# A post-norm attention block with a routed low-rank FFN on one core: group loop written out, last stage as one pipeline

## The chip, the cores and the metric

One core of one Trainium2 chip runs the whole program in one launch. The metric is the device time in microseconds (us). The kernel before takes 2026.87 us, the median of three runs (2025.49 to 2027.67). The execution that the profiler recorded took 2023.68 us; from its first instruction to its last are 2021.7 us (the span), and 2.0 us lie around that.

## What is computed

The reference, cut to what matters (one sequence of 1024 rows, width 512, 32 query heads of 128, 8 key/value heads):

```python
q, k, v = x @ w_q, x @ w_k, x @ w_v            # 32, 8 and 8 heads of 128
lk, lv = (x @ w_lq) @ w_lk, x @ w_lv           # 32 latent heads
q, k, lk = rope(q), rope(k), rope(lk)
attn = causal_softmax(q k^T * SCALE) v         # k, v shared by 4 heads
lat  = causal_softmax(q lk^T * SCALE) lv
x = layernorm(x + attn @ w_o + lat @ w_lo)
logits = x @ route_w.T                         # 8 experts
route_weight = one_hot(argmax(logits)) * max(logits)
h  = x @ A                                     # 8 experts x rank 16 = 128 columns
x = layernorm(x + (route_weight * h) @ Bw)
```

## The kernel before

The work before the last stage goes over 8 groups (one key/value head each, `GROUPS`) and in each over 2 pairs of query heads (`PAIRS`). Products are made in three matmuls of high and low parts (helper `three`, lines 349 to 351). For each pair the kernel projects and rotates queries and latent keys, and then goes over 32 score tiles of 128 rows: TensorE makes scores and transposes probabilities (line 435), VectorE takes row maxima (line 782) and low parts (line 724), ScalarE exponentials and high parts (line 551), GpSimd normalises probabilities (line 712) and makes low parts of weights (line 688). At a pair's end `outputs` multiplies the heads' results by `w_o` and `w_lo` for 8 row tiles of 128 rows (12 matmuls each); VectorE adds each to `acc`, which holds the residual, from PSUM (line 831).

The loop over the groups is a loop of the hardware on each engine (`sp.Fori`, `pe.Fori` and so on, line 486 for TensorE): the body stands in the program once, at its end is a compare and a branch, and the counts to wait for are worked out by register instructions from the group's number. Each engine runs its own list of instructions in the order in which the code writes them; semaphores join the lists. Nothing else orders the work.

What stands behind the loop, the last stage, runs in sections. VectorE waits until all 8 row tiles have been added, takes mean and variance of rows (`bn_stats`, line 845, `bn_aggr`, line 844), and makes 1/sqrt(variance + eps) from ScalarE's square root (line 643) by a reciprocal and one Newton step, four small instructions (lines 858 to 862), in two halves of 4 row tiles. It normalises the row tiles itself (line 870). TensorE transposes them (line 521), ScalarE copies that to SBUF (line 650), and TensorE makes logits and `h` together, 136 columns a row (line 529). When all 8 are there, VectorE makes the routing weights for the 8 row tiles in seven small instructions (lines 893 to 899) and weighs `h` (line 901). TensorE transposes the weighed rows (line 539), ScalarE copies (line 657), TensorE multiplies by `Bw` (line 544), VectorE adds (line 908), and the second norm goes as the first, again in two halves. SyncE stores each row tile when it is finished (line 340).

## Time and profile before

| | |
|---|---|
| median of the runs | 2026.87 us |
| the profiled execution | 2023.68 us |
| its span | 2021.7 us |
| TensorE busy with matmuls | 1979.0 us (98%), 12640 matmuls |
| VectorE busy | 1356.1 us (67%) |
| GpSimd busy | 1129.1 us (56%) |
| ScalarE busy | 1054.6 us (52%) |
| mean granted TensorE clock | 0.994 |
| chain that ended last | TensorE 97%, VectorE 1%, issue 1% |

Busy time counts instructions at work on data. Matmuls overlap, so the start of one to the start of the next says more than a duration: a matmul of 512 columns has a duration of 0.39 us, and the next starts 0.23 us after it. The last of the loop's matmuls starts at 1971.70 us, and the last stage fills the rest of the span.

### The profile page before, as it was taken

The numbers are of one execution on the slowest core, as the hardware profiler recorded it, in microseconds if no ns is written. First come the engines' busy times: TensorE is split into PE (matmuls) and PEld (weight loads), VectorE is DVE, ScalarE is ACT, GpSimd is POOL, SyncE is SP. The second block draws the span as 40 slices with busy tenths as digits, with TensorE's granted clock in tenths as the row PEclk, the third lists the DMA queues.
The fourth block names the chain that finished last, engine by engine and source line by source line (L and its number), as shares of the span: only waits on it lengthen the run. The fifth ranks groups of instructions, "written<-read, shape, count | busy, mean of one in ns | idle before, by whom it ended". The sixth has DMA issues, their size and how long they took to land.

```text
span 2021.7 us, 39463 instructions
## 1 busy us (share of the span) xinstructions
PE 1979.0 (98%) x12640; PEld 1806.8 (89%) x12640; DVE 1356.1 (67%) x3356; ACT 1054.6 (52%) x2445; POOL 1129.1 (56%) x905
## 2 busy tenths in 40 slices
PE   7999999999999999999999999999999999999994
PEld 6989989899898989989899898999989899898993
DVE  6758667585775747758476675757757586675756
ACT  3746627375372745728356372654727366272641
POOL 6637476374664647556465664646566374763730
PEclk9999999999999999999999999999999999999997
DMA  5010010101000010000100001010010100100001
GB/s 177 12 35 1 23 36 12 35 1 43 15 22 24 2 57 1 22 24 3 55 1 22 24 22 36 1 45 1 23 36 12 35 1 23 36 13 21 2 12 42
DMA packets 19366, 50.85 MB, mean 25 GB/s; under 512 B 5824, under 2 KB 7872, under 8 KB 19008
## 3 DMA queue, kind: packets, MB, share of 16 engines
q1 hardware_dynamic: 18992, 45.90, 6.8%
q8 instruction: 119, 1.95, 0.4%
q10 hardware_dynamic: 144, 2.10, 0.2%
q14 instruction: 111, 0.91, 0.2%
HBM read 45.89 MB, written 2.10 MB: 24 GB/s over the span
## 4 chain that ended last, share of the span: by engine, by line
PE 97%; DVE 1%; issue 1%; POOL 0%; DVEq 0%; POOLq 0%; ACT 0%; ACTq 0%
PE ps L349 28%; PE ps L350 28%; PE ps L351 28%; PE ps L435 13%; DVE stats L845 0%; PE ps L529 0%; PE ps L544 0%; PE ps L521 0%; DVE acc L870 0%; POOL pt_lo L688 0%; DVE acc L908 0%; DVE stats L844 0%; POOL mask L678 0%; DVE neg_max L782 0%; DVE acc L831 0%
## 5 line engine op out<-in xcount | busy, mean ns | idle before, releaser
L712 POOL TENSOR_TENSOR probs<-probs,inv_sum 128x640 f32<-128x640 f32 (+7 forms) x512 | 582.9, 1150 | 343.9 <-DVE inv_sum L789 342.9
L782 DVE CUSTOM_DVE_ANT_0 probs<-ps,mask 128x640 f32<-128x640 f32 (+7 forms) x512 | 384.3, 753 | 167.2 <-PE ps L351 121.1
L724 DVE TENSOR_TENSOR pt_lo<-ps,pt_hi 128x512 fp32r<-128x512 f32 (+3 forms) x768 | 399.0, 547 | 75.1 <-ACT pt_hi L551 73.2
L551 ACT ACTIVATE pt_hi<-ps 128x512 fp32r<-128x512 f32 (+3 forms) x768 | 347.0, 487 | 164.0 <-PE ps L435 160.8
L580 ACT ACTIVATE probs<-probs,neg_max 128x640 f32<-128x640 f32 (+7 forms) x512 | 397.0, 776 | 60.5 <-DVE neg_max L782 49.3
L349 PE MATMUL ps<-pt_hi,val_hi 128*128 128x256 f32 x1216 | 353.8, 291 | 0.0
L350 PE MATMUL ps<-pt_lo,val_hi 128*128 128x256 f32 x1216 | 342.7, 282 | 0.0
L351 PE MATMUL ps<-pt_hi,val_lo 128*128 128x256 f32 x1216 | 342.5, 282 | 0.0
L435 PE MATMUL ps<-ident,probs 128*128 128x128 f32 x2304 | 334.4, 273 | 0.0
L703 POOL TENSOR_TENSOR probs<-probs 128x512 f32<-128x512 f32 x144 | 186.7, 1296 | 198.9 <-DVE probs L758 198.9
L435 PEld LDWEIGHTS ps<-ident,probs 128*128 128x128 f32 x2304 | 271.9, 140 | 23.6
L551 ACT ACTIVATE ql_hi<-probs 128x512 fp32r<-128x512 f32 x128 | 80.9, 632 | 403.5 <-POOL probs L703 403.5
L350 PEld LDWEIGHTS ps<-pt_lo,val_hi 128*128 128x128 f32 x1216 | 232.2, 191 | 0.6
L349 PEld LDWEIGHTS ps<-pt_hi,val_hi 128*128 128x128 f32 x1216 | 231.9, 191 | 0.6
L351 PEld LDWEIGHTS ps<-pt_hi,val_lo 128*128 128x128 f32 x1216 | 231.6, 190 | 0.0
L688 POOL TENSOR_TENSOR pt_lo<-raw,pt_hi 128x1024 fp32r<-128x1024 f32 (+1 forms) x48 | 96.8, 2030 | 241.2 <-ACT pt_hi L551 241.2
L349 PE MATMUL ps<-val_hi,ql_hi 128*128 128x512 f32 x512 | 202.7, 396 | 0.0
L351 PE MATMUL ps<-val_hi,ql_lo 128*128 128x512 f32 x512 | 199.7, 390 | 0.0
L350 PE MATMUL ps<-val_lo,ql_hi 128*128 128x512 f32 x512 | 199.6, 390 | 0.0
L831 DVE TENSOR_TENSOR acc<-ps,acc 128x512 f32<-128x512 f32 x128 | 85.3, 688 | 153.4 <-PE ps L351 153.4
L724 DVE TENSOR_TENSOR ql_lo<-ps,ql_hi 128x256 fp32r<-128x256 f32 x256 | 105.0, 414 | 106.7 <-ACT ql_hi L551 103.3
L707 POOL TENSOR_TENSOR ql_lo<-probs,ql_hi 128x512 fp32r<-128x512 f32 x128 | 166.5, 1300 | 7.8 <-ACT ql_hi L551 7.8
(100 smaller groups left out, 4025.6 us busy)
## 6 DMA issues: line engine op xcount, KB each, us to landing
raw<-wo SPq DMA_DIRECT2D x32, 512.0 KB, 3.4
raw<-wq SPq DMA_DIRECT2D x16, 512.0 KB, 3.8
raw<-wlv SPq DMA_DIRECT2D x16, 512.0 KB, 3.6
raw<-wkv SPq DMA_DIRECT2D x8, 512.0 KB, 3.6
acc<-xT SPq DMA_DIRECT2D x4, 512.0 KB, 6.2
wlk_raw<-wlk SPq DMA_DIRECT2D x16, 128.0 KB, 3.0
acc<-x ACTq DMA_DIRECT2D x1, 2048.0 KB, 8.8
out<-acc SPq DMA_DIRECT2D x8, 256.0 KB, 2.4
```

Of the source, the lines that this page charges most:

```text
L349: pe.matmul(dst, ah, bh, start=first, stop=False, skip_group_check=True)
L350: pe.matmul(dst, ah, bl, start=False, stop=False, skip_group_check=True)
L351: return pe.matmul(dst, al, bh, start=False, stop=last, skip_group_check=True)
L435: mm = pe.transpose(ps[:, T_BANKS[u % len(T_BANKS)], P * (b - b0):P * (b - b0) + P], probs_of(n)[:, P * b:P * b + P], ident[:])
L551: return nc.scalar.activation(dst, src, ACT.Copy)
L580: nc.scalar.activation(dst, dst, ACT.Exp, bias=neg_max[:, n % 8:n % 8 + 1], scale=-1.0, accum_out=row_sum[:, n % 8:n % 8 + 1]).then_inc(q[ ...
L688: nc.gpsimd.tensor_tensor(l, raw_part(name), h, ALU.subtract).then_inc(q["w_lo_pool"], 1)
L703: nc.gpsimd.tensor_tensor(b[:, 0:512], b[:, 0:512], b[:, 512:1024], ALU.add).then_inc(q["rope_add"], 1)
L707: nc.gpsimd.tensor_tensor(l, probs[:, slot_of_rope(pair, r - 1), 0:512], h, ALU.subtract).then_inc(q["rope_lo"], 1)
L712: nc.gpsimd.tensor_tensor(b, b, inv_sum[:, k % 8:k % 8 + 1].to_broadcast([P, b.shape[-1]]), ALU.mult).then_inc(q["normed"], 1)
L724: return nc.vector.tensor_tensor(dst, src, h, ALU.subtract)
L782: nc.vector.tensor_tensor_reduce(out=probs_of(n).rearrange("p (b n) -> p b n", b=b), in0=scores_of(n), in1=mask[:, S - w:S].rearrange("p ( ...
```

## The change

Four things change:

- `Fori` becomes a Python `for`: the 8 groups stand in the program one after the other on all five engines. There is no branch, and each wait has a constant, so the register instructions are gone.
- The rows are taken in the order in which their outputs come (`OUT_ORDER`, `row(y)`), in three batches (`BATCHES`): y = 0 to 3, 4 and 5, 6 and 7. Norm, logits, routing and FFN of a batch start when that batch is there. The last two outputs (y = 6, 7) of the last pair are taken out of the loop and stand in pieces between the steps of the first batch.
- Rows are normalised by ScalarE (`normalize`: activation Identity with a bias and a scale for each partition), in place of VectorE's instruction of line 870. VectorE makes the bias, -mean/std, in one more small instruction for each batch (`scale6`).
- Buffers in PSUM: x and weighed rows are transposed into banks 4 and 5; logits and `h` go to banks 6, 7, 2, 3; FFN products to 0, 1, 6, 7. The copy of the logits to SBUF (line 893) is dropped; the routing reads PSUM.

The diff, cut:

```diff
-LN_TILES = ST // 2
+BATCHES = ((0, 1, 2, 3), (4, 5), (6, 7))
...
-            with pe.Fori(0, GROUPS) as g:
+            for g in range(GROUPS):
...
+                        if (g, pair) == (GROUPS - 1, PAIRS - 1) and y == 6:
+                            break
...
+            turn_x1(0, "pt_lo_made", GROUPS * PAIRS * T_UNITS)
+            turn_x1(1, "pt_lo_made", GROUPS * PAIRS * T_UNITS)
+            outputs(*last, 6, 0, 1)
+            mix(0)
+            turn_x1(2, "x1T_made", 1)
+            mix(1)
+            turn_x1(3, "x1T_made", 2)
+            outputs(*last, 6, 1, 2)
+            mix(2)
+            mix(3)
+            outputs(*last, 6, 2, 4)
+            outputs(*last, 7, 0, 2)
+            turn_wh(0, "x1T_made", 3)
+            turn_wh(1, "x1T_made", 4)
+            turn_x1(4, "whT_made", 1)
+            turn_x1(5, "whT_made", 2)
+            outputs(*last, 7, 2, 4)
+            ffn(0)
+            ffn(1)
+            turn_wh(2, "x1T_made", 5)
+            turn_wh(3, "x1T_made", 6)
+            mix(4)
+            mix(5)
+            ffn(2)
+            ffn(3)
+            turn_wh(4, "whT_made", 3)
+            turn_wh(5, "whT_made", 4)
+            turn_x1(6, "whT_made", 5)
+            turn_x1(7, "whT_made", 6)
+            ffn(4)
+            mix(6)
+            mix(7)
+            ffn(5)
+            turn_wh(6, "x1T_made", 7)
+            turn_wh(7, "x1T_made", 8)
+            ffn(6)
+            ffn(7)
...
+            def normalize(norm, y):
+                act.wait_ge(q[f"chain{norm}"], 6 * (batch_of(y) + 1))
+                nc.scalar.activation(row(y), row(y), ACT.Identity, bias=shift[:, y:y + 1], scale=rstd[:, y:y + 1]
+                                     ).then_inc(q["x1_made" if norm == 1 else "finished"], 1)
```

Of the helpers, `turn_x1(y)` is 4 transposes, `mix(y)` the 4 matmuls for logits and `h`, `turn_wh(y)` one transpose, `ffn(y)` the product with `Bw`; on VectorE `add_last(y)` and `add_ffn(y)` are the adds into `acc`, `spread` is `bn_stats`, `moments` the `bn_aggr` of a batch with the eps added, `scale1` to `scale6` and `route1` to `route6` are single small instructions, and `weigh(y)` is the product with the routing weights.

On TensorE the loop's end before: the last matmuls of the body, the branch, and then the last stage, all transposes and `mix`.

```order
L349 MATMUL ps<-val_hi,ql_hi 128x512
L350 MATMUL ps<-val_lo,ql_hi 128x512
L351 MATMUL ps<-val_hi,ql_lo 128x512
L486 REGISTER_ALU
L486 COMPARE_AND_BRANCH
L521 MATMUL ps<-ident,acc 128x128 [waits x1_made]
L521 MATMUL ps<-ident,acc 128x128 x3
L521 MATMUL ps<-ident,acc 128x128 [waits x1_made]
L521 MATMUL ps<-ident,acc 128x128 x3
L521 MATMUL ps<-ident,acc 128x128 [waits x1T_made,x1_made]
L521 MATMUL ps<-ident,acc 128x128 x3
L529 MATMUL ps<-raw,probs 128x136 [waits x1T_made,out_added,ffn_in]
```

In the changed program the first group's last matmuls are followed at once by the second group's first (`x_hi` with the query weights):

```order
L385 MATMUL ps<-val_hi,ql_hi 128x512
L386 MATMUL ps<-val_lo,ql_hi 128x512
L387 MATMUL ps<-val_hi,ql_lo 128x512
L385 MATMUL ps<-x_hi,pt_hi 128x512 [waits w_lo_pool]
L386 MATMUL ps<-x_lo,pt_hi 128x512
L387 MATMUL ps<-x_hi,pt_lo 128x512
L385 MATMUL ps<-x_hi,pt_hi 128x512
```

The branch is gone. Further on, behind the outputs of y = 5 of the last pair, TensorE has the first transposes of normalised rows, with the three matmuls of one step of y = 6 in between:

```order
L385 MATMUL ps<-val_hi,ql_hi 128x512
L386 MATMUL ps<-val_lo,ql_hi 128x512
L387 MATMUL ps<-val_hi,ql_lo 128x512
L557 MATMUL ps<-ident,acc 128x128 [waits pt_lo_made,x1_made]
L557 MATMUL ps<-ident,acc 128x128 x3
L557 MATMUL ps<-ident,acc 128x128 [waits pt_lo_made,x1_made]
L557 MATMUL ps<-ident,acc 128x128 x3
L385 MATMUL ps<-val_hi,ql_hi 128x512 [waits out_added]
L386 MATMUL ps<-val_lo,ql_hi 128x512
L387 MATMUL ps<-val_hi,ql_lo 128x512
L568 MATMUL ps<-raw,probs 128x136 [waits x1T_made,o_lo_made,ffn_in]
L568 MATMUL ps<-raw,probs 128x136 x3
```

All 24 matmuls of the outputs of y = 6 and 7 now stand behind the first transposes of normalised rows.

On VectorE before, behind the 8 adds of the last pair, stand the statistics of a half:

```order
L798 REGISTER_ALU
L798 COMPARE_AND_BRANCH
L845 BN_STATS stats<-acc 128x6 [waits out_added]
L845 BN_STATS stats<-acc 128x6 x3
L844 BN_AGGR stats<-stats 128x2 [waits ln_chain]
L844 BN_AGGR stats<-stats 128x2 x3
L852 TENSOR_SCALAR ve<-stats 128x4 [waits ln_chain]
L845 BN_STATS stats<-acc 128x6 x4
L844 BN_AGGR stats<-stats 128x2 [waits ln_chain]
L844 BN_AGGR stats<-stats 128x2 x3
L852 TENSOR_SCALAR ve<-stats 128x4 [waits ln_chain]
L858 RECIPROCAL rstd<-root 128x4 [waits root_made]
```

In the changed program the same engine, at the place where the second batch's routing begins (y = 7's add `L914`, FFN adds `L956`, statistics `L961`):

```order
L914 TENSOR_TENSOR acc<-ps,acc 128x512 [waits out_mm]
L961 BN_STATS stats<-acc 128x6 [waits out_added]
L956 TENSOR_TENSOR acc<-ps,acc 128x512 [waits y_mm] x2
L961 BN_STATS stats<-acc 128x6 [waits y_added] x2
L914 TENSOR_TENSOR acc<-ps,acc 128x512 [waits out_mm]
L961 BN_STATS stats<-acc 128x6 [waits out_added]
L1015 TENSOR_REDUCE top<-ps 128x2 [waits route,logits_mm]
L968 BN_AGGR stats<-stats 128x2 [waits stats1]
L968 BN_AGGR stats<-stats 128x2
L970 TENSOR_SCALAR ve<-stats 128x2 [waits moments1]
L1020 TENSOR_TENSOR cos_t<-ps,top 128x16 [waits route]
L984 RECIPROCAL rstd<-root 128x2 [waits chain1,root1]
```

The add of y = 7 and its statistics now stand behind the first two FFN adds and their statistics, and the second batch's routing (`L1015`, `L1020`) and the third batch's norm (`L968`, `L970`, `L984`) are laced together.

On ScalarE before, the last stage: a table load, two roots, copies, two roots.

```order
L643 ACT_TABLE_LOAD
L643 ACTIVATE root<-ve 128x4 [waits ve_made] x2
L650 ACTIVATE probs<-ps 128x512 [waits x1_turned] x6
L650 ACTIVATE probs<-ps 128x512 [waits logits_mm,x1_turned] x2
L657 ACTIVATE probs<-ps 128x128 [waits wh_turned,logits_mm]
L657 ACTIVATE probs<-ps 128x128 [waits wh_turned]
L657 ACTIVATE probs<-ps 128x128 [waits y_mm,wh_turned] x6
L643 ACTIVATE root<-ve 128x4 [waits ve2_made] x2
```

In the changed program, the part from the third batch's first root to the second norm's second root (`L721` is `normalize`, `L728` and `L734` are the copies):

```order
L734 ACTIVATE probs<-ps 128x128 [waits wh_turned] x2
L728 ACTIVATE probs<-ps 128x512 [waits x1_turned] x2
L717 ACTIVATE root<-ve 128x2 [waits ve1]
L734 ACTIVATE probs<-ps 128x128 [waits wh_turned]
L734 ACTIVATE probs<-ps 128x128 [waits y_mm,wh_turned] x3
L721 ACTIVATE acc<-acc,shift,rstd 128x512 [waits chain1] x2
L728 ACTIVATE probs<-ps 128x512 [waits logits_mm,x1_turned] x2
L717 ACTIVATE root<-ve 128x4 [waits ve2]
L734 ACTIVATE probs<-ps 128x128 [waits y_mm,wh_turned] x2
L717 ACTIVATE root<-ve 128x2 [waits ve2]
L721 ACTIVATE acc<-acc,shift,rstd 128x512 [waits chain2] x4
```

Roots, copies and normalised rows are laced on one engine. The root that waits for `ve1` now stands ahead of the copies that TensorE's FFN products wait for.

## Rows read from the trace of the kernel before

**Rows 1.** Busy time by stretches of the end; columns: stretch, length, engines, clock, DMA.
```profile
1972.10:1980.40 8.30, 0.00 (x0) 0.00 (x0) 7.93 (x26) 0.41 (x2) 0.00 (x0) 0.65 0.00 0
...
2009.00:2018.60 9.60, 0.05 (x1) 0.00 (x0) 9.03 (x28) 0.20 (x1) 0.00 (x0) 0.67 0.35 130
```
**Rows 2.** What TensorE waited for: total us, times, longest us.
```profile
PE ps L521 <- DVE acc L870: 8.4, 1, 8.4
...
PE ps L349 <- issue: 3.5, 7, 0.9
PE ps L349 <- POOL pt_lo L688: 2.6, 1, 2.6
```
**Rows 3.** TensorE in order of time, one branch: start, duration, instruction, idle before.
```profile
751.71 0.39 PE L350 MATMUL ps<-val_lo,ql_hi 128*128 128x512 f32 x1
751.94 0.39 PE L351 MATMUL ps<-val_hi,ql_lo 128*128 128x512 f32 x1
752.60 0.49 PE L349 MATMUL ps<-x_hi,pt_hi 128*128 128x512 f32 x1 [0.27 <-issue]
752.93 0.39 PE L350 MATMUL ps<-x_lo,pt_hi 128*128 128x512 f32 x1
```
**Rows 4.** Busy time by stretches: one without a branch; TensorE is first.
```profile
510.00:750.00 240.00, 239.70 (x1547) 220.14 (x1546) 163.25 (x405) 129.75 (x302) 140.91 (x112) 1.00 0.06 20
```
**Rows 5.** TensorE in order of time, the last stage.
```profile
1966.48 0.39 PE L349 MATMUL ps<-val_hi,ql_hi 128*128 128x512 f32 x1
...
1986.33 0.60 PE L521 MATMUL ps<-ident,acc 128*128 128x128 f32 x4
1986.77 1.09 PE L529 MATMUL ps<-raw,probs 128*128 128x136 f32 x8
...
1997.83 1.02 PE L544 MATMUL ps<-raw,probs 128*128 128x512 f32 x2
1998.69 0.27 PE L539 MATMUL ps<-ident,raw 128*128 128x128 f32 x1
```
**Rows 6.** VectorE in order of time, the last stage.
```profile
1957.89 1.88 DVE L831 TENSOR_TENSOR acc<-ps,acc 128x512 f32<-128x512 f32 x3
...
1972.85 2.47 DVE L845 BATCH_NORM_STATS2 stats<-acc 128x6 f32<-128x512 f32 x4
...
1979.04 0.16 DVE L859 TENSOR_TENSOR newton<-rstd 128x4 f32<-128x4 f32 x1
1979.24 0.16 DVE L860 TENSOR_TENSOR newton<-newton,ve 128x4 f32<-128x4 f32 x1
...
1994.11 0.22 DVE L894 TENSOR_REDUCE top<-cos_t 128x8 f32<-128x64 f32 x1
...
1995.65 1.67 DVE L901 TENSOR_TENSOR raw<-ps,cos_t 128x128 f32<-128x128 f32 x8
...
2016.65 1.91 DVE L870 TENSOR_SCALAR acc<-acc,stats,rstd 128x512 f32<-128x512 f32 x4
```
**Rows 7.** ScalarE's groups by shape: busy us, mean ns of one, idle before.
```profile
L551 ACT ACTIVATE ql_hi<-probs 128x512 fp32r<-128x512 f32 x128 | 80.9, 632 | 403.5 <-POOL probs L703 403.5
...
L580 ACT ACTIVATE probs<-probs,neg_max 128x512 f32<-128x512 f32 x64 | 46.1, 720 | 17.1 <-DVE neg_max L782 17.1
...
L650 ACT ACTIVATE probs<-ps 128x512 f32<-128x512 f32 x8 | 4.8, 598 | 7.7 <-PE ps L521 7.7
L657 ACT ACTIVATE probs<-ps 128x128 f32<-128x128 f32 x8 | 2.1, 277 | 9.4 <-PE ps L539 9.4
...
L643 ACT ACTIVATE root<-ve 128x4 f32<-128x4 f32 x4 | 0.8, 205 | 29.4 <-DVE ve L852 29.4
```
**Rows 8.** Busy time by stretches around the second norm; the clock is the number behind POOL's.
```profile
2002.90:2005.40 2.50, 0.01 (x1) 0.01 (x1) 2.43 (x9) 0.48 (x2) 0.00 (x0) 1.00 0.01 3
2005.40:2008.80 3.40, 3.38 (x4) 1.17 (x4) 1.16 (x2) 0.00 (x0) 0.00 (x0) 0.50 0.00 0
```
**Rows 9.** The page's DMA queues: packets, MB, share of 16 engines.
```profile
q8 instruction: 119, 1.95, 0.4%
```

More of the change, by code:

```diff
@@ L485, in _ @@
             pe.wait_ge(q["lq_lo_made"], 2)
[L486 removed]
+            for g in range(GROUPS):
                 for pair in range(PAIRS):
@@ new lines, in mix @@
+            def mix(y):
+                if y == 0:
+                    pe.wait_ge(q["ffn_in"], 32)
+                    pe.wait_ge(q["o_lo_made"], GROUPS * PAIRS * CHUNKS)
+                if y in (4, 6):
+                    pe.wait_ge(q["out_added"], SEED + GROUPS * PAIRS * ST - ST + (7 if y == 4 else 8))
+                pe.wait_ge(q["x1T_made"], y + 1)
+                for c in range(CT):
+                    mm = pe.matmul(mix_of(y), turned_x1(y)[:, P * c:P * c + P], ra[:, c, :], start=c == 0 and y % 2 == 0,
+                                   stop=c == CT - 1 and y % 2 == 1, skip_group_check=True)
+                mm.then_inc(q["logits_mm"], 1)
@@ new lines, in turn_wh, with ffn @@
+            def turn_wh(y, free, count):
+                pe.wait_ge(q["wh_made"], y + 1)
+                pe.wait_ge(q[free], count)
+                pe.transpose(ps[:, 4 + y % 2, 0:P], raw[:, 2, P * y:P * y + P], ident[:]).then_inc(q["wh_turned"], 1)
+            def ffn(y):
+                if y < 2:
+                    pe.wait_ge(q["out_added"], SEED + GROUPS * PAIRS * ST - ST + 5 + y)
+                elif y >= 4:
+                    pe.wait_ge(q["y_added"], y - 3)
+                pe.wait_ge(q["whT_made"], y + 1)
+                pe.matmul(y_of(y), turned_wh(y), raw[:, 1, 0:D], start=True, stop=True).then_inc(q["y_mm"], 1)
@@ L603, in _ @@
             nc.scalar.dma_start(acc[:], x).then_inc(q["res_in"], 16)
-            with act.Fori(0, GROUPS) as g:
+            for g in range(GROUPS):
                 for pair in range(PAIRS):
@@ L796, in output_lo, with add_output @@
                 lo(l, product_of(n), h).then_inc(q["o_lo_made"], 1)
-            with dve.Fori(0, GROUPS) as g:
+            def add_output(g, pair, y):
+                dve.wait_ge(q["out_mm"], SEED + per_pair(g, pair, ST, y + 1))
+                nc.vector.tensor_tensor(row(y), ps[:, y % 4, :], row(y), ALU.add).then_inc(q["out_added"], 1)
+            for g in range(GROUPS):
                 for pair in range(PAIRS):
@@ L889, in _ @@
-            chain = [0]
-            dve.wait_ge(q["logits_mm"], ST)
-            mix = ps[:, 4:8, :].rearrange("p b (y n) -> p (b y) n", y=2)
-            logits, equal, ranked, first, weight = (route[:, i] for i in range(5))
-            step(nc.vector.tensor_copy(logits, mix[:, :, 0:E]))
-            step(nc.vector.tensor_reduce(top[:], logits, AX.X, ALU.max))
-            step(nc.vector.tensor_tensor(equal, logits, top[:, :, None].to_broadcast([P, ST, E]), ALU.is_equal))
-            step(nc.vector.tensor_tensor(ranked, equal, order[:, None, :].to_broadcast([P, ST, E]), ALU.mult))
@@ L915, in _, with add_last, add_ffn @@
-            finish(ln2, 1)
+                    if (g, pair) != (GROUPS - 1, PAIRS - 1):
+                        for y in range(ST):
+                            if g == 0 and pair == 0 and y == 0:
+                                dve.wait_ge(q["res_in"], 16)
+                            add_output(g, pair, y)
+            def add_last(y):
+                add_output(GROUPS - 1, PAIRS - 1, y)
+            def add_ffn(y):
+                dve.wait_ge(q["y_mm"], y + 1)
+                nc.vector.tensor_tensor(row(y), y_of(y), row(y), ALU.add).then_inc(q["y_added"], 1)
@@ new lines, in spread, with moments @@
+            def spread(norm, y):
+                dve.wait_ge(q["out_added" if norm == 1 else "y_added"], (SEED + GROUPS * PAIRS * ST - ST if norm == 1 else 0) + y + 1)
+                nc.vector.bn_stats(stats[:, y, 0:6], row(y)).then_inc(q[f"stats{norm}"], 1)
+            def moments(norm, b):
+                ys = in_batch(b)
+                dve.wait_ge(q[f"stats{norm}"], ys.stop)
+                for y in BATCHES[b]:
+                    nc.vector.bn_aggr(stats[:, y, 6:8], stats[:, y, 0:6]).then_inc(q[f"moments{norm}"], 1)
+                dve.wait_ge(q[f"moments{norm}"], ys.stop)
+                nc.vector.tensor_scalar(ve[:, ys], stats[:, ys, 7], EPS, None, ALU.add).then_inc(q[f"ve{norm}"], 1)
@@ new lines, in _ @@
+            spread(2, 1)
+            add_last(7)
+            spread(1, 7)
+            route1(1)
+            moments(1, 2)
+            route2(1)
+            scale1(1, 2)
+            route3(1)
+            scale2(1, 2)
+            route4(1)
+            scale3(1, 2)
+            route5(1)
+            scale4(1, 2)
+            route6(1)
+            scale5(1, 2)
+            weigh(4)
+            scale6(1, 2)
+            weigh(5)
+            add_ffn(2)
+            add_ffn(3)
+            spread(2, 2)
```

356 lines of the change are left out of this document (230 added, 126 removed).

## The prediction

> **What bounds the kernel now.** I read the page's busy shares first: TensorE is busy 98% of the span, and the chain that ended last is 97% TensorE. So up to the last matmul of the loop only two things can move the time: TensorE's work, which the change leaves as it is, and holes in it. Next the waits of TensorE [rows 2] and the busy time by stretches. Over 240 us without a branch TensorE lacks 0.30 us [rows 4]; there is nothing to win there. Seven times, once for each jump back to the loop's head, it stops with the releaser "issue", 3.5 us in all [rows 2]. Then the end: from 1972.1 to 1980.4 TensorE does nothing while VectorE makes the first norm [rows 1], which is the wait of 8.4 us on the normalised rows [rows 2]; from 2009.0 to 2018.6 only VectorE works [rows 1]. The last normalised row is written at 1.91 + 2016.65 = 2018.56 [rows 6], and stores fill the 3.1 us to 2021.7. So the last stage is bound by a chain that goes to and fro between the engines, and the loop by TensorE.
>
> **The change, part by part.**
>
> The branch. The last matmul of a group starts at 751.94 and the next at 752.60 [rows 3]: 0.66 where matmuls of this size follow each other by 0.23 (751.71 to 751.94), so 0.43 lost; the one behind it comes after 0.33, another 0.10. The profile's "idle" of 0.27 there is this 0.43 less the modelled end of a matmul, 0.39 - 0.23 = 0.16. Over seven jumps that makes 3.5 [rows 2] + 7 x (0.16 + 0.10) = 5.3 us. It all stands on the path, since TensorE has its operands. With the code written out there is no jump: -5.3. Bounds: -3.5 (the idle alone) and -5.3 less another 2, if VectorE's, ScalarE's and GpSimd's missing register instructions also shorten the short waits of TensorE inside a group.
>
> The entry. TensorE waits 2.6 us for the first low parts of weights [rows 2]. ScalarE and SyncE set up registers before the instructions that lead there; I take 0.3 off this wait, an estimate between 0 and 0.6. Taken: -0.3.
>
> The end, as a chain in the time of before. Prices, each as the distance from one start to the next when engines are full: add 0.60 (3 in 1.88, the last 0.69 long), `bn_stats` 0.60 (4 in 2.47), small VectorE instructions that follow each other through a semaphore 0.20 (1979.04 to 1979.24), routing instructions 0.22 long, so 0.25, weighing 0.20 (8 in 1.67) [rows 6]. TensorE: 4 transposes 0.44 (1986.33 to 1986.77), `mix` 1.09 long, so 0.93, `ffn` 0.86 (1997.83 to 1998.69) [rows 5], a transpose of a weighed row 0.11, an output's 12 matmuls 12 x 0.23 = 2.72; a result is there some 0.16 after the engine is free. ScalarE: copy of x 0.60, of a weighed row 0.28, root 0.21 [rows 7]; queued ones overlap by about 0.1. From one engine to another 0.04.
>
> The one price that no row shows is ScalarE's normalising instruction, with a pointer for the bias and one for the scale. A copy of 512 columns without pointers takes 0.632, an exponential of 512 with a pointer for its bias 0.720 [rows 7]. One pointer is then 0.088 at most, and a second as much: 0.81, 0.71 when queued. Bounds: 0.54 (VectorE's own in line 870, from 4 in 1.91 [rows 6]) and 0.90. ScalarE's table holds, since the program has no more table loads than before.
>
> The Trainium skill ("ScalarE: Activation LUTs", "What ACT_TABLE_LOAD costs") states 186 ns + 0.833 ns a column, and some 93 ns more for each pointer: 0.80 us here. It speaks against this part of the change, since VectorE does the same in 0.54; the rows agree with its first pointer, and no row of this profile has two. By 0.72, the price of one pointer alone, the end would come 0.9 us earlier than below.
>
> 1. TensorE leaves the outputs of y = 5 at 1966.48 [rows 5]. The outputs of y = 3 left it 2 x 2.72 earlier, at 1961.04, so their add starts at 1961.24; with it, two statistics still due and the moments (0.60 + 1.20 + 0.6) VectorE is at 1963.7, and with the root and six small instructions (0.28 + 6 x 0.20) at 1965.2. ScalarE normalises four rows (4 x 0.71) and copies the first: `mix(0)` starts at 1968.7. TensorE fills all but 0.7 of that with transposes and one step of y = 6.
> 2. From there it is full until `ffn(1)`: 4 mix 3.72, 4 times 4 transposes 1.76, the other 21 output matmuls 4.76, two transposes of weighed rows 0.22, two ffn 1.72, a wait of 0.4 for the copies, 0.2 to the result: 1981.5. The routing of the first batch hides beside the outputs of y = 6 and 7.
> 3. VectorE: adds and statistics of FFN rows 0 and 1 come before the add of y = 7, then its statistics and the third batch's moments: 0.60 + 1.20 + 0.73 + 0.71 + 0.48 = 3.7 (the last is the moments: aggregates and eps, each behind a semaphore), to 1985.2.
> 4. ScalarE's root of the third batch stands ahead of the copies of weighed rows 2 and 3; they and `ffn(2)` wait for it: 0.56, to 1985.8. TensorE is idle for 2.4 us here. This is the wait that the change makes anew.
> 5. `ffn(2)`, `ffn(3)`, two transposes 2.0; two copies and two normalised rows 1.9: 1989.7. Transposes, `ffn(4)`, `mix(6)`, `mix(7)` 3.4: 1993.1. Six routing instructions and one weighing 1.8: 1994.9. Transpose, copy 0.65, `ffn(6)`, `ffn(7)` 1.9: 1997.4.
> 6. Add, two statistics, moments 2.55: 2000.0. ScalarE's root comes behind the normalised rows 0 to 3, then four more, 4 x 0.71: with the root 3.25, to 2003.25.
>
> Against 2018.56: -15.3. The stores stay, 3.1 us behind the last row. Where this gain comes from: the 8.3 and 9.6 us of VectorE alone [rows 1] become about 3 and 6, and in the chain from 1980 to 2009 the batches overlap. Sum: -5.3 - 0.3 - 15.3 = -20.9. The profiled execution's 2023.68 would be 2002.8; the median of the runs stands 3.2 above it, so **2006.0** is predicted.
>
> **Rivals.**
>
> *The clock falls in the new hole.* Before, TensorE stood idle for 2.5 us at a granted clock of 1.00, and the next 3.4 us, though full, were at 0.50 [rows 8], so 1.2 instead of 2.4 GHz. Step 4's hole is 2.4 us. For it: length. Against: the stretch of rows 8 came at the end of a stage in which TensorE had waited for others again and again; here it is full for over 14 us ahead of the hole (steps 1 and 2) and has 2 us of work right behind it. A stretch of 3.4 us at half rate, of which the matmuls on the chain are half, costs 1 to 2 us: about 2007.6.
>
> *More from the loop.* All register instructions on VectorE's and GpSimd's chains go; if TensorE's short waits inside the groups shrink with them, up to 2 us more: 2004.2. Against: rows 4 leave 0.30 us idle in 240.
>
> *Slower: straight code pays for fetching.* If each block of instructions fetched cost TensorE's queue what a jump costs, 119 fetches [rows 9] less the 8 at the loop's ends, by 5.3/7 = 0.76 each, would add 84 us: 2006 + 84 = 2090. It turns the result from 20.9/111 = 0.19 us a fetch. Against: a turn of the loop has 12640/8 = 1580 matmuls with as many weight loads, these packets are fetched in each turn of the loop already, and rows 4 have a full TensorE over them.
>
> *No gain at the end.* If the laced stage ran at half clock throughout, my chain would be 16 us longer, and 5.6 us of the branch and the entry remain less 0.7: 2022. Against: before the stage TensorE is full, and has only short holes in it.
>
> **How the numbers follow.** Forecast 0.62; clock falls once or twice 0.24; more from the loop 0.07; half clock throughout 0.03; fetching 0.02; 0.02 for a wait I have not seen. Runs of this kernel lie within 2.2 us, so 0.2% (4.1 us) is what can be told from no change. Faster: the first three and most of the last, 0.94. Same: half clock and the like, 0.03. Slower: 0.03. The range is the forecast with its bounds (1.9 less or 1.1 more for the normalising instructions, 2 either way for the branch, 2 for the handoffs between engines, of which the chain has some 25 at 0.04, in case one costs twice that and more), widened to the clock's case: 2002.0 to 2010.5.
>
> **What would show it.** Right: no "issue" among TensorE's waits; TensorE idle by less than 1 us between the last `outputs` and `mix`, one hole of 2 to 2.5 us behind `mix(5)` released by ScalarE's copy, and holes of about 1.3 and 1.2 ahead of `turn_x1(6)` and `turn_wh(6)`; Identity of 512 columns at 0.80; ScalarE full in the last 3 us before the last store. Wrong: TensorE losing starts at other places of the straight code; a clock of 0.5 in the stretch of the outputs of y = 6 and 7; a normalising instruction over 0.90; a span over 2006 or under 1997.

## The result and the profile after

The changed kernel takes **2005.88 us**, the median of four runs (2004.14 to 2007.88). The kernel before, run beside it, takes 2026.44 (2025.49 to 2027.67). The ratio is 0.9899 with a 95% interval of 0.9881 to 0.9916, so the change makes the kernel 20.6 us, or 1.0%, faster. The forecast was 2006.0 for the time and 20.9 for the gain. The time is inside the range and "faster" had 0.94.

The profiled executions tell less of a gain: 2023.68 before and 2007.88 after, with spans of 2021.7 and 2005.8. That is 15.9 and not 20.9, and the recorded limit for a wrong prediction, a span over 2006, was all but reached. Most of this text is on those 5 us.

The page after, for the waits and code loads that stood in [rows 2] and [rows 9]. First TensorE's waits (total us, times, longest us):

```profile
PE ps L385 <- DVE x_lo L838: 7.9, 1, 7.9
PE ps L385 <- POOL pt_lo L802: 4.7, 1, 4.7
PE ps L583 <- ACT probs L734: 2.1, 1, 2.1
...
PE ps L557 <- ACT acc L721: 1.1, 1, 1.1
PE ps L575 <- DVE raw L1048: 0.8, 1, 0.8
PE ps L568 <- ACT probs L728: 0.6, 1, 0.6
```

"Issue" is gone, and so is the 8.4 us wait on VectorE's normalised rows. The wait for the first low parts of the weights, 2.6 in [rows 2], is 4.7. The 2.1 us on ScalarE's copy in line 734 is the new hole that step 4 of the prediction named. Code loading, the queue of [rows 9] (packets, MB, share):

```profile
q8 instruction: 102, 1.67, 0.3%
```

102 packets against 119: the written-out program did not load more on this queue. The same 240 us of the middle as in [rows 4] (stretch, length, TensorE's busy time, and the other engines behind it):

```profile
510.00:750.00 240.00, 239.72 (x1547) 220.19 (x1546) 163.56 (x405) 129.57 (x302) 140.82 (x112) 1.00 0.06 21
```

TensorE lacks 0.28 us there and lacked 0.30 before. And a place where one group ends and the next begins, which answers to [rows 3] (start, duration, instruction):

```profile
752.89 0.39 PE L386 MATMUL ps<-val_lo,ql_hi 128*128 128x512 f32 x1
753.11 0.39 PE L387 MATMUL ps<-val_hi,ql_lo 128*128 128x512 f32 x1
753.34 0.39 PE L385 MATMUL ps<-x_hi,pt_hi 128*128 128x512 f32 x1
753.57 0.39 PE L386 MATMUL ps<-x_lo,pt_hi 128*128 128x512 f32 x1
```

The starts are 0.23 apart all the way through. With the jump, the last matmul of the group and the first of the next were 0.66 apart.

The last stage, TensorE in order of time (the number in brackets is idle time and what ended it); it answers to [rows 5]:

```profile
1978.08 1.88 PE L583 MATMUL ps<-raw,probs 128*128 128x512 f32 x4
1979.80 0.38 PE L575 MATMUL ps<-ident,raw 128*128 128x128 f32 x2
1980.02 2.02 PE L568 MATMUL ps<-raw,probs 128*128 128x136 f32 x16
1984.15 3.68 PE L583 MATMUL ps<-raw,probs 128*128 128x512 f32 x4 [2.11 <-ACT probs L734]
...
1989.17 1.36 PE L557 MATMUL ps<-ident,acc 128*128 128x128 f32 x8 [1.12 <-ACT acc L721]
...
1994.87 0.53 PE L575 MATMUL ps<-ident,raw 128*128 128x128 f32 x2 [0.78 <-DVE raw L1048]
```

The same four instructions of line 583, `ffn`, take 1.88 us at 1978.08 and 3.68 behind the hole at 1984.15. The clock tells why (stretch, length, TensorE, its loads, VectorE, ScalarE, GpSimd, then the granted clock):

```profile
1981.95:1984.10 2.15, 0.09 (x1) 0.00 (x0) 1.89 (x9) 0.38 (x3) 0.00 (x0) 1.00 0.00 0
1984.15:1987.60 3.45, 3.45 (x4) 1.35 (x5) 1.95 (x12) 0.11 (x1) 0.00 (x0) 0.51 0.00 0
```

TensorE stood idle at a granted clock of 1.00 and then worked at half of it, 1.2 GHz in place of 2.4. This is the first rival, "the clock falls in the new hole"; it happened in this execution.

ScalarE from there to the end, with line 721 the normalising, 717 the root and 734 the copies of weighed rows:

```profile
1983.72 0.20 ACT L717 ACTIVATE root<-ve 128x2 f32<-128x2 f32 x1 [6.18 <-DVE ve L970]
1983.83 0.42 ACT L734 ACTIVATE probs<-ps 128x128 f32<-128x128 f32 x2
...
1996.97 2.91 ACT L721 ACTIVATE acc<-acc,shift,rstd 128x512 f32<-128x512 f32 x4
2000.20 0.20 ACT L717 ACTIVATE root<-ve 128x2 f32<-128x2 f32 x1 [0.31 <-DVE ve L970]
```

The root that waits for VectorE until 1983.7 stands ahead of two copies whose transposes TensorE had finished by 1980.2 (1979.80 and 0.38 above), 3.5 us sooner. Before, VectorE normalised these rows, and the last stage ended with [rows 6]. Of the instruction that no row had priced, the group by shape (busy us, mean ns | idle before):

```profile
L721 ACT ACTIVATE acc<-acc,shift,rstd 128x512 f32<-128x512 f32 x16 | 11.8, 802 | 1.3 <-DVE shift L1009 1.2
```

0.802 us against 0.81 forecast, and the queued distance is (2.91 - 0.80)/3 = 0.70 against 0.71. The Trainium skill ("ScalarE: Activation LUTs", "What ACT_TABLE_LOAD costs") states 186 ns and 0.833 ns a column, and some 93 ns for each pointer, which makes an estimate of 0.80; this trace agrees.

### The profile page after: what moved, and what is told of

Same layout as the page of the kernel before. It is cut to its first block, busy times and chain, and to the rows that moved or that the text cites. A ratio compares the mean times of both kernels' runs of the same rounds, so it can differ in the third digit from the quotient of the medians.

```text
span 2005.8 us, 33652 instructions
## 1 busy us (share of the span) xinstructions
PE 1977.5 (99%) x12640; PEld 1806.8 (90%) x12640; DVE 1352.0 (67%) x3369; ACT 1064.1 (53%) x2463; POOL 1128.6 (56%) x905
## 4 chain that ended last, share of the span: by engine, by line
PE 88%; POOL 5%; DVE 4%; ACT 2%; issue 1%; SPq 1%; DMA 0%; ACTq 0%; DVEq 0%; POOLq 0%
PE ps L385 25%; PE ps L387 25%; PE ps L386 25%; PE ps L471 13%; POOL probs L817 3%; POOL ql_lo L821 2%; DVE probs L871 1%; DVE probs L870 1%; DVE probs L872 1%; ACT probs L656 1%; PE ps L583 0%; SPq L349 0%; ACT ql_hi L627 0%; DVE probs L896 0%; DVE val_lo L838 0%
## 5 line engine op out<-in xcount | busy, mean ns | idle before, releaser
L914 DVE TENSOR_TENSOR acc<-ps,acc 128x512 f32<-128x512 f32 x128 | 85.4, 687 | 144.2 <-PE ps L387 144.2
```

## Where the two profiled executions differ

Both spans cut at the same four places: the twelfth matmul of the loop over (the thirteenth starts), the start of the last matmul of the outputs of y = 5, the end of the last normalised row, the end. Each is read from the trace's instructions, in us from the start of the span.

| | before | after | difference | forecast |
|---|---|---|---|---|
| entry: to 12 matmuls into the loop | 23.01 | 26.03 | +3.0 | -0.3 |
| loop: from there to y = 5 | 1943.24 | 1938.42 | -4.8 | -5.3 |
| last stage: to the last row | 52.30 | 38.94 | -13.4 | -15.3 |
| stores | 3.1 | 2.4 | -0.7 | 0 |
| span | 2021.7 | 2005.8 | -15.9 | -20.9 |

The mechanism and the order of the sizes are there. Two things were against the changed kernel: an entry that is 3 us later, and 1.7 us lost to the clock behind the hole. Half of the 3 us is the clock too: the first matmul of the loop starts at 21.65 in place of 20.12, and the first twelve take 4.38 in place of 2.89. Theory A says that the late entry is a matter of the single execution, and that the profile of before had fallen on an early one (it lay 2.8 under the median of its runs). Theory B says that straight code makes the entry late, and a third possibility was that the load of x collides with the weights. The first four experiments and the second profile of before are for these.

## Experiments

All numbers are medians with the range of the runs in brackets, the ratio to the kernel before on the same chip with its 95% interval, and parts by the cuts of the table above. The kernel before had a median of 2025.81 beside the first four, of 2023.72 beside the four on the last stage's bound and the entry's loads, and of 2026.33 beside the last two, so medians from different groups are not comparable to better than 2 to 3 us; the parts read from the traces are.

**The changed kernel a second time, its two halves, and one load later.** No edit:

> The changed kernel once more, unaltered. Its profiled execution was 15.9 us shorter in span than the kernel before's, where 20.9 was forecast; 3.2 of the 5.0 us between lie at the entry: the first weights landed 1.4 us later than before, TensorE waited 4.7 us in place of 2.6 and then ran 3.4 us at the granted clock 0.50. Theory A (the entry is chance: which of the loads lands first): in this execution TensorE may wait under 3 us at the entry with the clock at 1.00, and then the span is near 2002; the times spread by 3 to 4 us. Theory B (the straight code makes the entry slower): TensorE waits over 4 us here too, and the span is near 2005.5.

Measured: 2005.66 (2004.12 to 2008.46), ratio 0.9906 [0.9891, 0.9922], span 2002.2. Its entry is over at 23.70, the last stage takes 37.25, and the clock doesn't fall behind the hole. The same code gives a span 3.6 us shorter: 2.3 of it is the entry and 1.7 the clock behind the hole, less 0.4 in the loop. Of theory A's two signs at the entry one came: the wait is 2.96, but the clock fell there too, 1.5 us behind the first matmul. The hole in the last stage is as long as in the first profile, but what follows is at full rate (columns as above):

```profile
1980.00:1982.10 2.10, 0.08 (x1) 0.00 (x0) 1.84 (x9) 0.33 (x3) 0.00 (x0) 1.00 0.00 0
1982.20:1985.60 3.40, 2.27 (x7) 1.03 (x8) 3.25 (x15) 1.39 (x5) 0.00 (x0) 1.00 0.00 0
```

The straight code alone, on the kernel before (the edit is the same on all five engines; besides, VectorE's wait for the load of x stands only in the first pair, as in the changed kernel):

```diff
-            with pe.Fori(0, GROUPS) as g:
+            for g in range(GROUPS):
```

> Only the five group loops are written out, the last stage is the kernel before's. The forecast's term for the seven jumps is 5.3 us, all on TensorE: no wait with the releaser issue is left, and the stretch from the first matmul of the first group to the last matmul of the last group is 5.3 us shorter (1951.58 us before, 1946.3 here), at whatever the entry costs. Theory A: 2021 us when the entry is as before, 2024 when the weights land late, so between 0.9973 and 0.999 of before. Theory B: the entry costs 3 us more each time, 0.999. A third, that straight code also shortens waits inside the groups, would make the stretch under 1945.

Measured: 2021.42 (2016.28 to 2025.14), ratio 0.9977 [0.9967, 0.9988], 4.4 us under the 2025.81 of before. Its loop takes 1938.41, as the changed kernel's, its last stage 52.8; its entry is over at 25.74.

The new end alone, with the loop kept over seven groups and the eighth, the same code, written behind it (on all five engines):

```diff
-            for g in range(GROUPS):
+            def group(g):
...
+            with pe.Fori(0, GROUPS - 1) as g:
+                group(g)
+            group(GROUPS - 1)
```

> The last stage of the change, with a hardware loop over the first seven groups and only the last group written out, so six jumps are left. By the forecast's terms the last stage gives 15.3 us and one jump 0.76, against before -16.1: 2010.4 us, and 4.5 us more than the changed kernel at an equal entry. The waits with the releaser issue are 6, some 3.0 us in all. If the gain were in the straight code, it would be near before. Theory B on the entry: the first wait is about 2.6 us here as in the kernel before, since the loop's code is the same there; theory A: it varies as in the others.

Measured: 2010.09 (2007.76 to 2012.03), ratio 0.9921 [0.9908, 0.9935], 15.7 under before. Its entry is over at 25.38, with a wait of 2.60. Six jumps are left and cost as before (total, times, longest):

```profile
PE ps L390 <- issue: 3.4, 6, 0.8
```

The halves give 4.4 and 15.7, together 20.1, and the whole kernel beside them 20.15. One jump, 0.6 to 0.8, is gone in both, and each interval is 2 to 3 us to either side; within that they add up, and neither hides the other.

The load of x into the accumulators, which starts at 15.3, put behind the weights of the first group:

```diff
-            nc.scalar.dma_start(acc[:], x).then_inc(q["res_in"], 16)
...
                     weights_hi(g, f"lv{pair}")
+                    if g == 0 and pair == 0:
+                        nc.scalar.dma_start(acc[:], x).then_inc(q["res_in"], 16)
```

> The changed kernel with ScalarE's load of the residual x (2 MB) put behind its high parts of the first pair's weights, so it no longer runs beside the first loads of weights. If that load is what makes the first weights land late (the memory queues moved 440 GB/s from 18 to 22 us in the changed kernel), they land by 16 us, TensorE's wait at the entry is under 3 us, the clock stays at 1.00, and the span is 2001 to 2002.5, the times 1 to 3 us under the changed kernel's with less spread. If the queue of loads ahead of them or the straight code is the cause, nothing changes: 2005.

Measured: 2006.37 (2003.95 to 2007.39), ratio 0.9901 [0.9886, 0.9916]; that load now starts at 20.5, the wait for the first low parts is 4.6 all the same, and the entry is over at 25.76. That load isn't what makes the weights late.

**Is the entry the straight code's?** The kernel before once more, with a profile:

> The kernel before, unchanged, profiled a second time. Its first twelve matmuls of the loop were over at 23.0 us of the span in the profile of the prediction, and at 23.7 to 26.2 in all six others with the same loads, one of which keeps the loops. Theory A (the entry is a matter of which transfers land first, the same for both kernels, and the first profile fell on an early one): this one has them over at 24 to 26, waits 3 to 4.7 us for the first low parts, and its time is 1 to 3 us above the 2023.68 of the first profiled execution. Theory B (straight code makes the entry later): again 23 and a wait of 2.6.

Measured: 2025.64 (2023.92 to 2027.19), ratio 1.0004 [0.9994, 1.0014] to itself; the profiled execution took 2026.23. The entry is over at 25.48, 2.5 later than in the profile that the prediction was made from. The first matmul of the loop in the first profile, in this one and in the changed kernel's first, and the stretch that begins there in this one:

```profile
20.12 0.50 PE L349 MATMUL ps<-x_hi,pt_hi 128*128 128x512 f32 x1 [2.65 <-POOL pt_lo L688]
21.08 0.79 PE L349 MATMUL ps<-x_hi,pt_hi 128*128 128x512 f32 x1 [2.60 <-POOL pt_lo L688]
21.65 0.76 PE L385 MATMUL ps<-x_hi,pt_hi 128*128 128x512 f32 x1 [4.67 <-POOL pt_lo L802]
```

```profile
21.00:24.40 3.40, 3.32 (x8) 2.64 (x9) 1.02 (x2) 0.14 (x1) 3.40 (x5) 0.50 0.96 343
24.40:27.00 2.60, 2.60 (x13) 2.12 (x12) 1.30 (x2) 0.00 (x0) 2.15 (x1) 0.99 0.82 298
```

The expectation was half right. The wait is 2.60, as in the first profile and not the 3 to 4.7 expected, but the first matmul comes a microsecond later and at half the clock, where the first profile's was at the full one (its first matmul took 0.50 us, this one 0.79). The length of the wait spoke for theory B: it is 2.60 to 2.65 in the three profiles with loops and 2.5 to 4.7 in the eight without (those with the tables first). But theory B's consequence, a late entry with straight code, falls: the entry of the kernel before is as late as the changed kernel's (23.70, 25.06 and 26.03 in its three profiles), and in the kernel with loops and the new end it was 25.38. The traces also show what the start of the first matmul hangs on. ScalarE makes the high part of the first query weights when these have landed and it is done with the high parts of the latent query, whichever is later; TensorE's first matmul follows 3.55 us later with loops and 3.7 without (us):

| | weights landed | latent query's parts done | ScalarE starts | first matmul | first twelve take |
|---|---|---|---|---|---|
| before, first profile | 16.54 | 16.36 | 16.57 | 20.12 | 2.89 |
| before, second | 16.35 | 17.38 | 17.53 | 21.08 | 4.40 |
| loops with the new end | 16.96 | 17.40 | 17.56 | 21.11 | 4.27 |
| changed, first profile | 17.84 | 15.87 | 17.95 | 21.65 | 4.38 |
| changed, second | 15.90 | 15.65 | 16.01 | 19.72 | 3.98 |
| changed, third | 17.08 | 16.81 | 17.19 | 20.90 | 4.16 |

So the wait is short with loops because the engines reach it later (the latent query's parts are done at 16.4 to 17.4 there, at 15.6 to 16.9 in the eight without), not because the weights land sooner. From this profile of before to the two others of the changed kernel the span falls by 21.9 and 21.0.

**What the last stage is bound by.** The rows normalised by VectorE again, in the new order:

```diff
+            def normalize(norm, b):
+                dve.wait_ge(q[f"chain{norm}"], 6 * (b + 1))
+                for y in BATCHES[b]:
+                    nc.vector.tensor_scalar(row(y), row(y), rstd[:, y:y + 1], shift[:, y:y + 1], ALU.mult, ALU.add
+                                            ).then_inc(q["x1_made" if norm == 1 else "finished"], 1)
```

> The changed kernel with its rows normalised by VectorE (16 TENSOR_SCALAR of 128x512 behind the sixth step of each scale chain, 0.54 us each by [rows of before], 0.48 queued) in place of ScalarE's 16 Identity ACTIVATEs of 0.83. Everything else is the changed kernel's. Theory A (the last stage's gain is the order: a third batch, the last two tiles behind the two short batches, three batches of norm 2): VectorE gets 7.7 us more work in a stage in which it is the engine with the least slack, but each batch saves the hop to ScalarE and 0.35 us a row; worked out through the chain of waits the two cancel, so the time is within 1.5 us of the changed kernel (2004.5 to 2007.5). Theory B (moving the normalising to ScalarE is a large part of the gain): undoing it costs 3 us or more, 2009 or later.

Measured: 2006.96 (2005.54 to 2008.39), ratio 0.9912 [0.9898, 0.9925]. Theory A's range held (its 0.83 for ScalarE's instruction was high, the traces have 0.80). The gain of the end comes from the rest of the new end, its order and batches and buffers; which of the two engines normalises is worth 0.3 to 1.3 us by the medians, which is less than the groups can be compared to. In the trace the last stage takes 40.8, where the first profile's took 38.9; both have the clock down behind the hole of 2.1, and this one a second time, in its last four instructions of `ffn`, which take 3.75 where the first profile's took 1.96, so that most of the 1.9 is the clock's. The price moved to another wait. Four rows of the second norm stand on VectorE ahead of the last weighing, and TensorE waits for that:

```profile
1990.89 1.92 DVE L994 TENSOR_SCALAR acc<-acc,rstd,shift 128x512 f32<-128x512 f32 x4
1992.92 0.49 DVE L1033 TENSOR_TENSOR raw<-ps,cos_t 128x128 f32<-128x128 f32 x2
```

```profile
PE ps L575 <- DVE raw L1033: 2.7, 1, 2.7
```

ScalarE's copies ahead of its root:

```diff
             copy_x1(5)
-            roots(1, 2)
             copy_wh(2)
             copy_wh(3)
+            roots(1, 2)
```

> Only ScalarE's order: the copies of mix tiles 2 and 3 (0.28 us each) ahead of the square root of the third batch, which waits for VectorE until 1983.7. They are ready at 1980.2, so ffn(2) and ffn(3) start without the 2.1 us hole behind mix(5). Theory A (the hole is what the clock falls in, and what stands behind it is bound by VectorE's third batch): the hole goes, with it the 3.4 us at half clock, which cost 1.7; the end moves by 0.6 for the order and up to 1.7 for the clock: 0.6 to 2.3 us earlier than the changed kernel, 2003.5 to 2005.3. Theory B (the end is set by PE's own work behind the hole): all of the 2.1 us and the clock's 1.7 come back, 3.5 us or more, under 2002.5. If the hole is only moved to the next wait (turn_x1(6), for the rows that VectorE's batch gives) the clock can fall there, and the time is the same within 0.6.

Measured: 2005.02 (2004.04 to 2006.54), ratio 0.9907 [0.9892, 0.9922]. By the times that can't be told from no change. By the trace the last stage takes 36.70, against 37.25 in the changed kernel's execution at full clock: 0.55 less, where 0.6 was expected for the order. The hole of 2.11 is gone, and most of it stands again one step on, where TensorE waits for VectorE's weighing:

```profile
1980.45 1.88 PE L583 MATMUL ps<-raw,probs 128*128 128x512 f32 x4
1983.78 0.60 PE L575 MATMUL ps<-ident,raw 128*128 128x128 f32 x2 [1.45 <-DVE raw L1048]
1985.44 1.36 PE L557 MATMUL ps<-ident,acc 128*128 128x128 f32 x8 [1.07 <-ACT acc L721]
```

So the hole showed the wait of the earliest waiter; the bound behind it is VectorE's third batch. This one was attacked next, by moving it ahead of work that isn't due (and, smaller, the routing and statistics around it and ScalarE's rows 6 and 7 ahead of its copies 4 and 5):

```diff
...
             spread(1, 6)
-            add_ffn(0)
-            add_ffn(1)
-            spread(2, 0)
-            spread(2, 1)
             add_last(7)
+            weigh(3)
             spread(1, 7)
-            route1(1)
+            add_ffn(0)
             moments(1, 2)
...
```

> Orders of VectorE and ScalarE alone (TensorE's is the changed kernel's): the last output row 7 is added and its norm and scale chain worked before the first FFN sums, the FFN sums and the statistics of norm 2 fill the waits behind, and ScalarE takes mix copies 2 and 3 ahead of the third square root and the rows 6 and 7 ahead of mix copies 4 and 5. Theory A (the last stage is bound by VectorE's order: row 7's product is ready at 1978.3 and VectorE is idle from 1976.1 to 1979.1, so the third batch's chain can end 2 us sooner, and the holes of 2.1 and 1.1 shrink): the last row ends 3.4 us earlier at full clock, and 1.7 more if the clock no longer falls: 3 to 5 us under the changed kernel, 2001 to 2003. Theory B (TensorE's work is the bound and the holes only move): within 1 us.

Measured: 2002.52 (2000.73 to 2002.89), ratio 0.9889 [0.9874, 0.9904]. The last stage takes 33.7, 3.6 less than the changed kernel's at full clock, against 3.4 expected. The copies' order of the experiment before is in it, 0.55 by itself; the other 3.0 belong to the moves together, which were not tried one by one. TensorE has no hole over 0.8 left in it, and ScalarE's root of the third batch runs at 1980.3 and not at 1983.7:

```profile
1981.38 1.88 PE L583 MATMUL ps<-raw,probs 128*128 128x512 f32 x4
1983.17 0.53 PE L575 MATMUL ps<-ident,raw 128*128 128x128 f32 x2
1984.02 0.63 PE L557 MATMUL ps<-ident,acc 128*128 128x128 f32 x4 [0.32 <-ACT probs L734]
```

```profile
1980.26 0.20 ACT L717 ACTIVATE root<-ve 128x2 f32<-128x2 f32 x1 [0.37 <-DVE ve L970]
```

**The entry.** The weights of the first group stand behind the tables on SyncE's queue. Here the key's and the first query's go ahead, and ScalarE takes the query's high part ahead of those of the latent query:

```diff
-            for slot, table in ((1, cos), (2, sin)):
...
                         sp.dma_start(raw_of(name), src).then_inc(raw_in[i % RAW_SLOTS], 16)
+                        if (g, pair, name) == (0, 0, "q0"):
+                            for slot, table in ((1, cos), (2, sin)):
...
+            weights_hi(0, "q0")
             for n in range(2):
                 act.wait_ge(q["lq_mm"], n + 1)
```

> The changed kernel with the loads of the first key and query weights issued ahead of the four loads of the cos and sin tables (1 MB in 4096 packets of 256 B), and ScalarE's high part of the first query weights ahead of the two of the latent query. Theory A (the entry waits for the first weights because they stand behind the tables on SP's queue): the weights land at about 9 instead of 17.9, the first matmul of the loop is then released by the latent query's low parts at 16.6 or by the tables, 17 to 18 instead of 19.7 to 21.7, and TensorE's idle time of 3.0 to 4.7 shrinks to under 1.5, so that the clock stays up over the first twelve matmuls, which gives another 1.1: 3 to 5 us under the changed kernel, 2001 to 2003. Theory B (the transfers share one rate: what goes ahead pushes the tables back by as much, and the tables' own transposes then wait): 0 to 1.5 us.

Measured: 2001.58 (2000.61 to 2003.03), ratio 0.989 [0.9874, 0.9905]. The median is 4.3 us under the changed kernel's first one, but the kernel before was at 2023.72 on this chip, so the ratios show 2 to 3 us; the last experiment below compares on one chip. The twelfth matmul is over at 20.65, 3 to 5.4 earlier than in the changed kernel's profiles. SyncE's issues in the changed kernel and in this one (start, duration, instruction):

```profile
3.08 3.34 SPq L349 DMA_DIRECT2D probs<-cos  x2
6.46 4.97 SPq L349 DMA_DIRECT2D probs<-sin  x2
11.48 1.20 SPq L353 DMA_DIRECT2D wlk_raw<-wlk  x1
12.72 0.43 SPq L369 DMA_DIRECT2D raw<-wq  x1
```

```profile
3.71 0.64 SPq L365 DMA_DIRECT2D raw<-wq  x1
4.40 1.41 SPq L370 DMA_DIRECT2D probs<-cos  x2
5.85 6.58 SPq L370 DMA_DIRECT2D probs<-sin  x2
```

The weights' load is issued 9 us earlier and lands at 11.6 (expected at about 9), in place of 17.8. What is left is a wait for the tables, the rival's part, of one microsecond (TensorE, in brackets), and the clock stays up behind it:

```profile
16.12 1.94 PE L408 MATMUL ps<-ident,probs 128*128 128x128 f32 x16 [0.97 <-DMA probs<-sin]
```

```profile
21.00:24.40 3.40, 3.40 (x18) 2.85 (x17) 2.84 (x5) 0.00 (x0) 3.40 (x3) 1.00 0.98 410
```

Matmuls of 512 columns start every 0.23 us in it, and every 0.43 at a clock of 0.50 in the second profile of before.

**All of it together**, and the changed kernel beside it. The edits of the last two, and the last row normalised by VectorE in place of ScalarE:

```diff
-            normalize(2, 7)
...
+            nc.vector.tensor_scalar(row(7), row(7), rstd[:, 7:8], shift[:, 7:8], ALU.mult, ALU.add).then_inc(q["finished7"], 1)
```

> The orders of e5_short_batch_first and the loads of e7_weights_first together, and the last row 7 normalised by VectorE (one TENSOR_SCALAR of 0.54) beside ScalarE's row 6. Theory A (the entry and the last stage are apart and add up): e7's 4.3 us and e5's 3.4 us under the changed kernel's median, and 0.7 of the last row by VectorE, 8.4 together: 1997.5 if all of it comes, and span 1994 to 1995. Theory B (the two medians were drawn from one spread of entries, since e5 and e7 were compared with one set of runs of before that was itself lower): the two share 2 us, 1999.5 or later, and the changed kernel run beside it falls under 2004.

Measured: **1997.94** (1997.81 to 2003.21; three of the four runs within 0.3), ratio 0.9869 [0.9853, 0.9886]. Theory A had 1997.5.

> The changed kernel once more, on the chip of the best one. Theory A: 2004 to 2007 as in its first two runs, with an entry that waits 3.0 to 4.7 us for the first weights. Theory B: under 2004. For the clock: of five executions with the 2.1 us hole behind the sixth mix, three fell to half the clock behind it and two did not; this one adds a sixth.

Measured: 2006.71 (2005.15 to 2010.65), ratio 0.9911 [0.9894, 0.9927]; entry over at 25.06, last stage 37.3, no fall of the clock behind the hole. The combination is 8.8 us under the changed kernel on the same chip: by the traces the entry is over 4.1 earlier (20.94) and the last stage is 4.3 shorter (33.0). Theory A holds. With the row on VectorE the last row ends 0.7 sooner than in the experiment with VectorE's new order, and the span gains nothing, for the stores then take 3.14 instead of 2.45.

## Why the prediction was right

*The jumps*, -5.3 forecast. The stretch between entry and last stage is 1943.24 and 1943.82 in the two profiles of before, 1942.98 with six jumps, and 1938.3 to 1938.8 in every kernel without any. That is 4.8 in the profiled pair and 4.4 to 5.5 over all, 0.64 to 0.79 a jump on average against 0.76. Single jumps differ more: counted by starts, as the prediction did for one, the seven of the first profile lose 0.55 to 1.17 each. The working by starts and not by the "idle" column was needed: the idle alone would have given 3.5. Of the 2 us more that the other engines' register instructions might have given nothing came; the rival "more from the loop" is refuted by the lack of 0.28 in 240 us, unchanged.

*The entry*, -0.3 forecast. No run shows a gain from register instructions that is clear of the spread: the latent query's parts are done somewhat earlier without loops, but from ScalarE's first high part to the first matmul it is 3.55 with loops and 3.7 without. What the term missed is the spread. The first profile of before was an early one, with its weights landed at 16.54 and, alone among the eleven profiles in which TensorE waits 2.5 us or more for them, with the clock up over the first twelve matmuls; in the other ten these take 3.98 to 5.26. The prediction had looked for a fall of the clock only in the new hole. Over the others there is no difference between the kernels that the spread of 2 to 3 us would show. The forecast's offset of 3.2 from the profiled execution to the median held this, as the second profile of before suggests (2.5 us later at the entry, 2026.23 in all), so the median came out right although the profiled pair is 5 us off. The term should have been given bounds from below zero to +3.

*The last stage*, -15.3 forecast: from the table's cut the forecast chain takes 37.0 (1966.26 to 2003.25), and measured are 37.2 to 37.3 at full clock and 38.9 with the clock's fall. The holes are at the places named: 0.55 ahead of the first `mix` (0.7 forecast), 2.11 behind `mix(5)` (2.4), 1.12 ahead of `turn_x1(6)` (1.3), 0.78 ahead of `turn_wh(6)` (1.2). The normalising instruction is 0.802 (0.81). Which part of the new end gives how much, the three batches, the outputs of y = 6 and 7 between them or the buffers, was not separated.

*The clock*, a rival with 0.24 and a price of 1 to 2 us. It fell in three of the seven executions profiled with this hole (the first one, with the later load of x, and with VectorE's rows; the expectation of the last run left out the kernel with loops, the seventh) and in none of the three whose longest hole is 1.45 or less. It costs 3.68 - 1.88 = 1.8 in `ffn`, of which 1.7 reach the end. Three of seven is more than 0.24, though seven executions are too few to tell the two apart; the argument against it in the prediction, 14 us of full work ahead of the hole, was no protection. The medians of the four runs don't tell such a fall from a late entry.

*Luck*: the forecast of 2006.0 is 0.1 from the median, and that is closer than its terms. The loop and the last stage at full clock gave up to 1 us less than forecast each, the stores 0.7 more, the clock's fall takes 1.7 in some executions and not in others, and the offset to the median was one number for a spread that nobody had looked into. The mechanism and the sizes of the two large terms were right; the last tenths were not foreseen.

*The stores*, 0 forecast, -0.7 measured: ScalarE finishes the last rows 0.70 apart where VectorE did so every 0.46, and in the combination, where rows 6 and 7 come from two engines, the stores take 3.14 again. That fewer stores under way together are the cause is likely but not shown.

*Fetching*, the rival on the other side (0.19 us a fetch would have turned the sign): 102 packets and a full TensorE; it doesn't occur.

*What stays open*: the entry is over at 23.0 to 25.5 in the two profiles of before and at 23.7 to 26.0 in the three of the changed kernel. The landing of the first query weights (15.9 to 17.8), the latent query's parts (done at 15.7 to 17.4) and the clock make this up, and with the weights issued ahead of the tables it is over at 20.65 and 20.94; which of the transfers ahead of them is late in a given execution, and why, was not separated.

## What to carry to other kernels

Before a term is read from one profiled execution, look how far that execution lies from the median of the runs, and ask which stretch could hold the difference; here the entry's 3 us hid in it. When a wait is closed and the end moves by a quarter of it, the next waiter's releaser is the bound: here the copy's hole of 2.1 us gave 0.55, and moving VectorE's third batch ahead of work that wasn't due, with that copy and some smaller moves, gave 3.6. At a kernel's start the load that the first big stage waits for belongs ahead of loads that hold the queue; here the issues of the four table loads held SyncE for 8.3 us.

## What the runs showed of the hardware that was not expected

- A loop's jump costs TensorE 0.64 to 0.79 us on average when its operands are there (single ones 0.55 to 1.17), and the waits put down to "issue" show 0.50 to 0.57 of it (3.5 us in seven, 3.4 in six, 4.0 in seven).
- The same hole of 2.1 us in TensorE, at a granted clock of 1.00, was followed by a stretch at 0.50 in three executions and at 1.00 in four. A hole of 2.6 at the entry likewise: at full clock in the first profile of before, at half in the second. Over all eleven profiles with a hole of 2.5 to 4.7 there the clock fell in ten, within the hole or up to 1.5 us into the work. The fall isn't decided by the length of the hole alone.
- The load of the first query weights (512 KB) took 7.9 us from issue to landing when it was issued at 3.7, behind the four loads of x and one of 128 KB, and 5.1 when issued at 12.7, behind the tables. It landed at 11.6 in place of 17.8: the place on the queue decided, not the time in flight.
- An Identity ACTIVATE of 128x512 with pointers for bias and scale takes 0.802 us, and 0.70 from start to start when queued.
